# Embedding rows of a small language-model tower: ten of 32 blocks picked by one-hot matmuls on TensorE, 22 gathered by GpSimd

## What is computed

```python
h = embed_table[x]                      # x: (8, 512) ids below 500, table (500, 256)
h = depthwise_conv(h, 31 taps) + conv_b # per channel, along the sequence, 'SAME'
h = h + linear_attention(layernorm(h))  # 16 heads of 64: softmax(q), softmax(k), two products, w_out, b_out
h = h + mixture_of_experts(layernorm(h))# 8 experts, the best 2 of each token, relu squared
```

## Time and profile before

| | us |
|---|---|
| median of 3 runs | 778.38 (777.66 to 778.66) |
| the profiled execution | 779.55 |
| its span, first to last instruction | 777.8 |
| PE busy | 635.4 (82%) |
| DVE busy | 472.2 (61%) |
| POOL busy | 336.8 (43%) |
| ACT busy | 311.6 (40%) |
| mean granted clock of TensorE | 0.929 |

### The profile page before, as it was taken

The page is one execution under the profiler, slowest core; times in us unless marked ns, Lnnn a source line. Parts: engine busy times, 40 slices in busy tenths (PEclk is TensorE's granted clock), DMA queues, the critical chain, the costliest instruction groups (busy, mean ns, idle before and its releaser), DMA issues. The chain is left out here.

```text
span 777.8 us, 16591 instructions
## 1 busy us (share of the span) xinstructions
PE 635.4 (82%) x4950; PEld 544.6 (70%) x4951; DVE 472.2 (61%) x1216; ACT 311.6 (40%) x667; POOL 336.8 (43%) x312
## 2 busy tenths in 40 slices
PE   0269487999999999999999997208998999988783
PEld 0169466788787878878788776106897888888673
DVE  0147476677879878797887874727443454444441
ACT  3123025335453443535335354015443454555552
POOL 6733223230723608155171735252443444454564
PEclk9779789999999999999999999557998999999997
DMA  7370586010111101111020101332452444465563
GB/s 240 120 200 1 108 264 217 1 55 2 56 55 46 66 1 66 43 54 54 22 88 0 54 27 56 108 116 69 71 83 47 78 68 77 73 103 88 92 102 43
DMA packets 38584, 60.57 MB, mean 78 GB/s; under 512 B 6282, under 2 KB 31890, under 8 KB 37906
## 3 DMA queue, kind: packets, MB, share of 16 engines
q1 hardware_dynamic: 23266, 36.80, 16.0%
q0 software_dynamic: 14976, 22.10, 15.2%
q10 hardware_dynamic: 288, 1.05, 0.4%
HBM read 30.54 MB, written 28.34 MB: 76 GB/s over the span
## 5 line engine op out<-in xcount | busy, mean ns | idle before, releaser
L1433 POOL DMA_INDIRECT out<-y,token_at x72 | 113.2, 1573 | 131.0 <-SPq L1413 130.4
L701 POOL DMA_INDIRECT queue_d<-row,slot x64 | 64.2, 1003 | 164.0 <-DVE slot L1013 147.0
L1513 DVE SCALAR_TENSOR_TENSOR act_w<-relu,queue_rows 128x512 f32<-128x512 f32 (+1 forms) x72 | 45.6, 634 | 116.0 <-ACT relu L1457 107.9
L1167 PE MATMUL bank<-xt_hi,w_first 128*128 128x512 f32 x256 | 94.2, 414 | 0.9 <-DVE second_half L891 0.9
L1167 PE MATMUL bank<-w_first,xt_hi 128*128 128x512 f32 x256 | 84.2, 410 | 2.4 <-DVE xt_lo L881 1.5
L693 POOL TENSOR_TENSOR second_half<-second_half,q_inv 128x512 f32<-128x512 f32 x64 | 64.9, 1042 | 42.7 <-DVE q_inv L900 42.5
L751 ACT ACTIVATE second_half<-second_half 128x512 f32<-128x512 f32 x64 | 40.3, 631 | 88.2 <-DVE second_half L891 87.9
L759 ACT ACTIVATE k_exps<-bank,k_negmax 128x512 f32<-128x512 f32 x64 | 44.3, 692 | 74.9 <-DVE k_negmax L907 74.8
L1555 PE MATMUL bank<-w_hi,a_hi 128*128 x224 | 70.6, 315 | 3.5 <-issue 2.7
L1555 PE MATMUL bank<-w_lo,a_hi 128*128 x224 | 63.9, 285 | 0.0
L1555 PE MATMUL bank<-w_hi,a_lo 128*128 x224 | 63.8, 285 | 0.0
(11 more groups left out here) (174 smaller groups left out, 1567.5 us busy)
## 6 DMA issues: line engine op xcount, KB each, us to landing
queue_rows<-queue_d SPq DMA_DIRECT2D x74, 129.0 KB, 2.1
store<-in_L_ffn_w SPq DMA_DIRECT2D x4, 1536.0 KB, 9.2
out<-res SPq DMA_DIRECT2D x8, 512.0 KB, 2.9
h_d<-store SPq DMA_DIRECT2D x7, 512.0 KB, 9.0
h_in<-h_d SPq DMA_DIRECT2D x7, 512.0 KB, 3.9
wqk<-in_L_attn_w_qkv SPq DMA_DIRECT2D x1, 2048.0 KB, 8.2
queue_d<-filler SPq DMA_DIRECT2D x1, 1290.0 KB, 11.7
out<-y,token_at POOLq DMA_INDIRECT x72, 3.9
```

The source lines that it names most:

```text
L701: pool.indirect_dma_start(out=queue_d, in_=row[:, t, c, :], in_offset=None, out_offset=bass.IndirectOffsetOnAxis(ap=slot[:, TT * c + t:TT ...
L1167: last = nc.tensor.matmul(o, a, c, start=(n == 1), stop=(n == 3 * len(pairs)))
L1433: pool.indirect_dma_start(out=out, in_=y[:, j % RING, :], in_offset=None, compute_op=ALU.add, out_offset=bass.IndirectOffsetOnAxis(ap=toke ...
L1513: nc.vector.scalar_tensor_tensor(out=act_w[:, u % 2, 0:width], in0=relu[:, u % 2, 0:width], scalar=rows[:, u, DIM:DIM + 1], in1=relu[:, u ...
```

## The change

The first 22 columns of the ids are gathered by GpSimd as before (`GATHERED = 22`). The last ten (`PICKED = 10`) are picked on TensorE:

- The whole table is loaded once into `words` (four chunks of 128 rows side by side, in the part of SBUF that `h` takes later), by two DMAs of ACT's queue. DVE first zeroes the last chunk, which holds only 116 rows.
- DVE converts the ids to float32 (`ids_f`). GpSimd's new iota writes `word_no[p, k] = p + 128 k`.
- For each picked column n, TensorE's `spread(n)` multiplies the column, repeated over 128 columns, with the identity, which puts the 128 ids in every partition of a bank (1 float32 product, 128 columns).
- DVE's `take_hot(n)` compares them with `word_no` for all four chunks at once: 128x512 one-hot values in `hot`, which has two buffers.
- TensorE's `pick(n)` adds up four float32 products of 256 columns, `hot` chunk by `words` chunk.
- DVE's `take_picked(n)` copies the 128x256 result from PSUM to `rows`.

All of this stands on TensorE and DVE ahead of the turning of `wv`. `turn(0)`, SP's load of `wqk` and what follows wait for 22 gathers instead of 32; TensorE also waits for the ten copies.

```diff
+VOCAB = 500
+VC = -(-VOCAB // P)
+PICKED = 10
+GATHERED = BLK - PICKED
...
+    spare = store[:].rearrange("p a n -> p (a n)")
+    words = spare[:, 0:VC * DIM].rearrange("p (k c) -> p k c", k=VC)
+    hot = spare[:, VC * DIM:VC * DIM + 2 * VC * P].rearrange("p (n k t) -> p n k t", n=2, k=VC)
+    ids_f = sbuf("ids_f", [P, BLK])
+    word_no = sbuf("word_no", [P, VC])
...
-            sp.wait_ge(gathered, 16 * BLK)
+            sp.wait_ge(gathered, 16 * GATHERED)
...
+            nc.gpsimd.iota(word_no[:], [[P, VC]], base=0, channel_multiplier=1,
+                           allow_small_or_imprecise_dtypes=True).then_inc(word_no_ready, 1)
             pool.wait_ge(ids_in, 16)
-            for i in range(BLK):
+            for i in range(GATHERED):
...
         def _(act):
+            act.wait_ge(words_zero, 1)
+            whole = VOCAB // P
+            act.dma_start(words[:, 0:whole], embeddings[0:whole * P].rearrange("(k p) c -> p k c", p=P)
+                          ).then_inc(words_in, 16)
+            act.dma_start(words[0:VOCAB - whole * P, whole], embeddings[whole * P:VOCAB]).then_inc(words_in, 16)
             act.wait_ge(taps_out, 32)
...
         def _(dve):
+            nc.vector.memset(words[:, VC - 1], 0.0).then_inc(words_zero, 1)
...
+            def take_hot(n):
+                dve.wait_ge(ids_spread, n + 1)
+                if n >= 2:
+                    dve.wait_ge(picked_psum, n - 1)
+                full = [P, VC, P]
+                nc.vector.tensor_tensor(hot[:, n % 2], bank[5 + n % 2][:, 0:P].unsqueeze(1).to_broadcast(full),
+                                        word_no[:].unsqueeze(2).to_broadcast(full), ALU.is_equal
+                                        ).then_inc(hot_ready, 1)
+
+            def take_picked(n):
+                dve.wait_ge(picked_psum, n + 1)
+                nc.vector.tensor_copy(rows[:, PICKED - 1 - n, :], bank[7 if n % 2 else 4][:, 0:DIM]
+                                      ).then_inc(picked, 1)
...
+            dve.wait_ge(ids_in, 16)
+            nc.vector.tensor_copy(ids_f[:], ids[:]).then_inc(ids_ready, 1)
+            dve.wait_ge(word_no_ready, 1)
+            take_hot(0)
+            for n in range(PICKED):
+                if n + 1 < PICKED:
+                    take_hot(n + 1)
+                take_picked(n)
...
+            def spread(n):
+
+                if n >= 2:
+                    pe.wait_ge(hot_ready, n - 1)
+                i = GATHERED + n
+                nc.tensor.matmul(bank[5 + n % 2][:, 0:P], ids_f[:, i:i + 1].to_broadcast([P, P]), ident[:],
+                                 start=True, stop=True).then_inc(ids_spread, 1)
+
+            def pick(n):
+                pe.wait_ge(hot_ready, n + 1)
+                if n >= 2:
+                    pe.wait_ge(picked, n - 1)
+                for k in range(VC):
+                    last = nc.tensor.matmul(bank[7 if n % 2 else 4][:, 0:DIM], hot[:, n % 2, k], words[:, k],
+                                            start=(k == 0), stop=(k == VC - 1))
+                last.then_inc(picked_psum, 1)
+
             pe.wait_ge(ident_ready, 1)
+            pe.wait_ge(ids_ready, 1)
+            spread(0)
+            spread(1)
+            pe.wait_ge(words_in, 32)
+            for n in range(PICKED):
+                pick(n)
+                if n + 2 < PICKED:
+                    spread(n + 2)
             pe.wait_ge(wv_in, 16)
...
+            pe.wait_ge(picked, PICKED)
...
-            pe.wait_ge(gathered, 16 * BLK)
+            pe.wait_ge(gathered, 16 * GATHERED)
```

More of the change, by code:

```diff
@@ L217, in convolve @@
     wv = h_in[:].rearrange("p b t c -> p (b t c)").rearrange("p (k n) -> p k n", k=KC)
+    spare = store[:].rearrange("p a n -> p (a n)")
[3 more added lines that the diff above has]
+    word_no = sbuf("word_no", [P, VC])
+    words_zero, words_in, ids_ready, word_no_ready, ids_spread, hot_ready, picked_psum, picked = (sem(n) for n in (
+        "words_zero", "words_in", "ids_ready", "word_no_ready", "ids_spread", "hot_ready", "picked_psum", "picked"))
     ids_in, taps_in, bias_in, wqk_in, wv_in, wo_in = (sem(n) for n in (
```

## The result

The changed kernel takes 782.28 us in the median of 20 runs, the one before 778.61: a ratio of 1.0046, 95% interval 1.0035 to 1.0057. It is slower by 3.7 us, where I forecast 14.0 us faster. The profiled execution has a span of 781.8 us, 4.0 more than before.

The account below looks back on a forecast made before the run. The prediction took GpSimd's gathers, which TensorE's sets wait for, as the bound. Ten fewer gathers (12.5 us) and a warm first set (1.5) gave 778.38 - 14.0 = 764.4 us, range 763.0 to 769.5.

Parts of the forecast that it names:

- Behind the sets nothing in the chain changes: Stages after the first: they keep the whole gain, with later cold starts worth some 0.7 us either way.
- The rival that I set on the slower side: First stage: TensorE stays at 1.2 GHz through the picks, sets start 4.7 us later than before, 783 us; chance 0.05.
- Ten gathers removed, 12.5 us: First stage, GpSimd: the 22nd gather is the last and lands at 32.3 instead of 44.79, 12.5 us earlier.
- What hangs on the gathers moves with them: SP, ACT and GpSimd work behind G, the last gather's landing (32.3), moves as one piece; cost 0.
- When the picks begin, 5.9: First stage, TensorE: the table is in at 5.6 and the first pick starts at 5.9.
- TensorE's cost, 23.0 us at the high clock: First stage: picks, spreads, hand-overs and transposes, plus 2.2 to 3.5 us for a slow clock; TensorE free at 31.1 to 32.4.
- DVE covered: Pick loop: DVE needs 1.1 to 1.5 us plus 0.2 a period against TensorE's 2.0, so TensorE sets the period.
- The sets start warm, 1.5 us: Start of the sets: after a gap of about 1 us TensorE's clock is still 1.00; the first set gains 1.5 us.
- my rival of a clock that falls again ahead of the sets: Start of the sets: picks end early or transposes count for nothing, 765.9 us; chance 0.06.
- The clock and transposes: Ahead of the sets: transposes keep the clock high, against the skill's rule, by which the gain would be 12.5, not 14.0.
- DVE holding up the gathers: First stage, rival: DVE's pick instructions block GpSimd's gathers, losing 11.1 of the 12.5 us, 777 us; chance 0.05.
- The threshold of the slow rival: First stage: picks at the low clock become the bound from 3.55 us a pick on.

Follow-up runs that it names:

- e4: The kernel before with 22 gathers and the other ten blocks zeroed by one DVE memset, without picks; ratio 0.9826 to the kernel before.
- e5: The changed kernel with 24 small products at TensorE's start, so that attention's loop begins at instruction 2096; 765.34 us, ratio 0.9841 to the kernel before.
- e1: The kernel before with 210 semaphore increments ahead of TensorE's wait for the gathers, loop at instruction 2001; ratio 1.0575 to the kernel before.
- e6: The kernel before with 52 small products at TensorE's start, loop at instruction 1998; ratio 1.0233 to the kernel before.
- e7: The kernel before with 64 small products at TensorE's start, loop at instruction 2046; ratio 1.0002 to the kernel before.
- e8: The changed kernel with 17 small products at TensorE's start and 14 transposes in the gap before the sets, loop at 2096; ratio 0.9838 to the kernel before.
- e10: The kernel before with 44 small products at TensorE's start, loop at instruction 1966; ratio 1.0120 to the kernel before.
- e3: The kernel before with 100 semaphore increments ahead of TensorE's wait for the gathers, loop at instruction 1891; ratio 1.0158 to the kernel before.

## Why the prediction was wrong

**The step that failed** is the last of the sum: "Behind the sets nothing in the chain changes". It held for the first 12.5 us of it: the sets moved by 12.63 us, the first batch of attention by 12.54, and e4 and e5 show that the whole program would have followed. What I left out was that the change lengthens TensorE's instruction stream ahead of a loop. I costed each added instruction by its time and its waits, and none by its place. The two jumps back cost 16.8 us (8.45 and 8.38), which turned a gain of 12.5 into a loss of 4. e1 and e6 make the same loss from the kernel before with none of the change's work; e5 takes it out of the changed kernel with all of its work left in.

The rival that I set on the slower side was the wrong mechanism. It had the picks at the low clock, ending at 45.9, and TensorE free at 49.5; they ended at 27.7 (24.09 + 3.62), and TensorE was free at 29.67. The sign came out as in that rival, but not one row of it did. No rival of mine had a loss behind the first stage.

A page of the Trainium skill had a warning: "Runtime: NRT & Kernel Launch", on instruction fetch mechanics, says that each engine's instruction memory is refilled in 16 KB blocks of 256 instructions, that TensorE's holds 2048 instructions, and that a taken branch to a target outside the current window of two such blocks stalls until it is fetched. This case's traces agree with the block (16 KB packets, a period of 256 in e7) and with a stall at a jump. They don't agree with the window of two: the loop spans at least seven blocks and jumps back without a fetch in the kernel before. The place where the limit falls is the runs' own: between 1743 and 1786 instructions, not 2048. By that page a loop of 1644 instructions after an insertion of 210 was a thing to look at.

Point by point, in the prediction's order:

- *Ten gathers removed, 12.5 us:* right. 44.79 to 32.16 is 12.63, and e4 gives 13.5 us in the runs, with an interval of 11 to 16.
- *What hangs on the gathers moves with them:* right, up to the loop. The load of wqk, ACT's split and banded 2 and 3 held nothing up. (Set 8 starts at G + 20.3 by my own terms, 3.7 and seven times 2.37, not at G + 20.7; it is covered either way.)
- *When the picks begin, 5.9:* it was 6.78. The taps came half a microsecond later (3.97 in place of 3.48), and with them DVE's masks and ids.
- *TensorE's cost, 23.0 us at the high clock, and a free TensorE at 31.1 to 32.4:* the size of a period was right (1.95), the loss at the start too large. TensorE's first work was at 5.06, and from the second pick on, at 10.44, the products took 379 ns as in the earlier trace rows. The first pick took 3.61 us against 1.89, a loss of 1.7 us where I had 2.2 to 3.5. The granted clock can't be used here: it reads 1.00 from 4.5 us on, through products that took twice as long. The 16 transposes of wv took 1.91 us where I had 2.4. TensorE was free at 29.67, 2.49 us before the gathers.
- *DVE covered:* right. take_hot measured 0.68 and take_picked 0.42.
- *The sets start warm, 1.5 us:* wrong for the changed kernel. The gap grew from the 1 us that I expected to 2.49, because the picks ended early, and the clock fell at 34.0, with TensorE at work again for 1.8 us. The set took 5.39 us, no better than the 5.25 of before. In kind this is my rival of a clock that falls again ahead of the sets. e8 shows that the step is real when the gap is filled.
- *The clock and transposes:* in e8 14 transposes and those of wv fill the time ahead of the sets, and the first set runs at the high clock. The Trainium skill's rule that transposes don't count as activity ("TensorE: Matmul & The Clock Gate", the part on the PE-mode transpose) is not borne out by it, as the prediction had it: in e5 the clock had fallen 3.8 us after the last product (28.49 to 32.3), and in e8 it held for 5.4 us with transposes alone (28.53 to 33.97).
- *DVE holding up the gathers:* did not happen. The steps stayed at 1.25.
- *The threshold of the slow rival:* (44.8 - 5.9 - 3.6) / 10 is 3.53, not 3.55; nothing hangs on it.

My range ended at 769.5 and left 5 in 100 for slower. Both were worked out from the stage that I had looked at. Nothing in it covered a stage in which the code is the same.

## What to carry to other kernels

Before an edit adds instructions to an engine whose stream holds a long loop, count the loop's instructions and where it begins in the 16 KB pieces of the fetch, and compare the packets of the instruction queue with the stream's length: here more packets than pieces meant that a loop was fetched again at each turn. If it is, some dozens of cheap instructions in idle time ahead of the loop can be worth more than the change itself (here 16 us of 782, e5 against the changed kernel). And when a gain goes missing, line up one instruction per batch in both traces: a steady difference with steps names the place in minutes.

## What the runs showed of the hardware

- TensorE ran a loop of 1644 instructions without fetching it again as long as it lay in about seven pieces of 256 instructions; beyond that nine pieces came anew in each later turn, not only the missing one, for 5.5 to 8.5 us a jump. The standstill was 3.3 (e10) to 5.5 us (e1) of it; in the changed kernel the clock's fall that follows made up most of the rest.
- A semaphore increment in TensorE's own stream cost about 0.16 us (17.2 us for the 110 by which e1 and e3 differ). Twenty-four float32 products of 8 columns, 95 instructions with their weight loads, took 1.36 us in e5.
- The granted clock can fall while TensorE is already at work again: in the changed kernel at 34.0, after a gap that had ended at 32.16.
